# Output rows of a fused attention and ternary feed-forward kernel: the layer norm's gain applied with the deviation, its spread moved into the quantisation scalars, one step less between stages

## The reference

```python
z = out @ Wout
xh = (z - mean(z)) * rsqrt(var(z) + 1e-5) * g_out
act_scale = 127.0 / max(max(abs(xh)), 1e-5)
x_dq = clip(round(xh * act_scale), -128, 127) / act_scale
x = x + x_dq @ w.T + bias
```

## Time and profile before

| | |
|---|---|
| time, median of 3 runs | 1786.67 us (1785.74 to 1787.05) |
| the profiled execution's own time | 1786.81 us |
| its span, first to last instruction | 1784.5 us |
| TensorE busy | 1604.5 us, 90% |
| GpSimd busy | 1421.9 us, 80% |
| VectorE busy | 1407.2 us, 79% |
| ScalarE busy | 1141.8 us, 64% |

### The profile page before, as it was taken

How to read it: one execution, slowest core, us unless ns; L and a number is a source line. 1 busy time by engine, 2 the same in 40 slices (tenths; PEclk the granted TensorE clock), 3 DMA queues, 4 the chain that set the end, 5 groups by cost and what they waited for, 6 DMA issues and landing times.

```text
span 1784.5 us, 46777 instructions
## 1 busy us (share of the span) xinstructions
PE 1604.5 (90%) x15122; PEld 1079.6 (60%) x15122; DVE 1407.2 (79%) x2569; ACT 1141.8 (64%) x2195; POOL 1421.9 (80%) x934
## 2 busy tenths in 40 slices
PE   3786897899999999998995898799999999998997
PEld 1443554577777777776552455477777777776553
DVE  4885898788888888884765798688888888887576
ACT  1342555587787788777441555477887887787441
POOL 3564666799999999997673566799999999999574
PEclk9998999899999999998997999899999999999998
DMA  6000012011112111100023002021111111110023
GB/s 186 1 0 21 25 29 59 13 37 35 28 37 49 25 37 37 29 21 14 30 71 102 25 29 65 1 47 26 38 37 25 37 37 41 26 32 13 7 71 100
DMA packets 41302, 68.84 MB, mean 39 GB/s; under 512 B 8880, under 2 KB 9392, under 8 KB 41136
## 3 DMA queue, kind: packets, MB, share of 16 engines
q1 hardware_dynamic: 36512, 58.12, 13.3%
q10 hardware_dynamic: 4640, 8.54, 1.4%
HBM read 58.11 MB, written 8.54 MB: 37 GB/s over the span
## 4 chain that ended last, share of the span: by engine, by line
PE 44%; issue 26%; POOL 17%; DVE 9%; ACT 1%; DVEq 1%; POOLq 1%; DMA 1%; SPq 0%; ACTq 0%
PE ps L1162 21%; PE ps L1135 10%; PE ps L1138 10%; DVE work L930 5%; POOL rinv L491 4%; POOL work L496 4%; POOL work L523 3%; POOL qo L454 2%; POOL work L541 2%; PE ps L1204 1%; DVE work L958 1%; POOL rstd L486 1%; DVE denom L955 1%; POOL work L498 1%; POOL work L462 1%
## 5 line engine op out<-in xcount | busy, mean ns | idle before, releaser
L511 POOL TENSOR_TENSOR work<-work 128x1024 f16<-128x1024 f32 (+2 forms) x576 | 978.2, 1733 | 44.2 <-ACT work L644 41.6
L930 DVE SCALAR_TENSOR_TENSOR work<-ps,tab 128x1024 f32<-128x1024 f32 (+3 forms) x640 | 668.7, 1059 | 141.3 <-PE ps L1138 139.4
L644 ACT ACTIVATE work<-work 128x1024 f32<-128x1024 f32 (+3 forms) x640 | 578.2, 924 | 207.3 <-DVE work L930 203.4
L1162 PEld LDWEIGHTS ps<-vals,work 128*128 128x128 bf16 (+1 forms) x8704 | 545.3, 98 | 115.8 <-POOL work L511 2.2
L1162 PE MATMUL ps<-vals,work 128*128 128x129 f16 x8704 | 600.5, 221 | 1.9 <-POOL work L511 1.8
L1135 PE MATMUL ps<-qo,kT 128*128 128x512 f16 (+3 forms) x1280 | 344.2, 351 | 20.8 <-DVE work L930 15.0
L1138 PE MATMUL ps<-qo,kT 128*128 128x512 f16 (+3 forms) x1280 | 342.1, 349 | 0.0
L1106 PE MATMUL ps<-wq,work 128*128 128x512 f16 x768 | 178.0, 390 | 20.4 <-DVE work L863 20.4
L1138 PEld LDWEIGHTS ps<-qo,kT 128*128 128x128 f16 x1280 | 123.2, 98 | 117.5 <-issue 3.3
L1204 PE MATMUL ps<-wout,work 128*128 128x512 f16 x768 | 175.0, 385 | 0.0
L1106 PEld LDWEIGHTS ps<-wq,work 128*128 128x128 f16 x768 | 74.6, 100 | 113.5 <-issue 34.2
(11 more groups left out here) (131 smaller groups left out, 1727.0 us busy)
## 6 DMA issues: line engine op xcount, KB each, us to landing
tab<-bias_table SPq DMA_DIRECT2D x64, 512.0 KB, 4.7
work<-in_x SPq DMA_DIRECT2D x32, 256.0 KB, 2.6
tab<-in_x SPq DMA_DIRECT2D x32, 256.0 KB, 2.7
out_x<-work ACTq DMA_DIRECT2D x32, 256.0 KB, 2.2
work<-in_L_cond_Wq SPq DMA_DIRECT2D x1, 2048.0 KB, 12.8
work<-in_L_cond_Wout SPq DMA_DIRECT2D x2, 1024.0 KB, 10.3
qo<-in_L_cond_w SPq DMA_DIRECT2D x1, 1024.0 KB, 9.5
qo<-in_L_cond_b SPq DMA_DIRECT2D x2, 256.0 KB, 4.2
```

Of the source, the lines that this page charges most:

```text
L511: pool.tensor_tensor(low[:, k % LRING, :, c0:512], probs[:, r, :, c0:512], high[:, r, :, c0:512], ALU.subtract).then_inc(low_pool, 1)
L644: act.activation(probs[:, k % RING, :, c0:512], probs[:, k % RING, :, c0:512], ACT.Exp).then_inc(expd, 1)
L930: dve.scalar_tensor_tensor(out=probs[:, k % RING, :, c0:512], in0=ps[:, 2 * (k % 2):2 * (k % 2) + 2, c0:512], scalar=SCORE, in1=tab[:, :, ...
L1162: last = pe.matmul(ps[:, sum_bank(i, q), (t % SUMS) * VS:(t % SUMS + 1) * VS], parts[:, rings[part], e, s * P:(s + 1) * P], vals[:, j, :], ...
```

## The change

`c_norm` becomes one instruction that subtracts the mean from the PSUM bank and multiplies by g_out, and writes y directly. GpSimd's `c_gain` and the buffer zn go. y is now larger than before by the factor sqrt(var + eps), and so is its largest magnitude. Two one-number operations take rstd in: `amx` is max(amax * rstd, 1e-5), the same number as before, and `ascale` is 127 / amx * rstd. `c_power` also waits until the scale of the tile two before has been made, since that now reads the rstd buffer.

On VectorE `c_norm` is put right behind `c_stat`, and `c_quant` of the same tile goes at the end of the same step. The lags from `c_quant` on fall by one: quantisation 4 to 3, `c_turn_y` 5 to 4, `c_ternary` 6 to 5, `c_final` 7 to 6, `c_resid` 6 to 5, the store 8 to 7.

```diff
--- before.py
+++ after.py
...
-        zn = carve(work, D)
         y = carve(work, 2, D)
...
@@ -527,19 +526,15 @@
 
                 def c_power(t, u):
                     pool.wait_ge(c_ve, NT * b + t + 1)
+                    pool.wait_ge(c_as, NT * b + t + 1)
                     pool.tensor_tensor(rstd[:, u, :], ve[:, u, :], minus_half[:, 0:1],
                                        ALU.pow).then_inc(c_rstd, 1)
-
-                def c_gain(t, u):
-                    pool.wait_ge(c_zn, NT * b + t + 1 + 2)
-                    pool.wait_ge(c_y1, NT * b + t + 1)
-                    pool.tensor_tensor(y[:, u, :], zn, gout_b[:, :], ALU.mult).then_inc(c_y, 1)
 
                 def c_resid(t, u):
                     pool.wait_ge(c_xr[u], 8 * (NT * b + t - u) + 16)
                     pool.wait_ge(c_fin, NT * b + t + 1)
                     pool.tensor_tensor(xb[:, u, :], x_re[:, u, :], fbias_b[:, :], ALU.add).then_inc(c_xb, 1)
-                skewed(pool, NT, [(c_power, 3), (o_lows, 0), (c_gain, 3), (c_resid, 6)])
+                skewed(pool, NT, [(c_power, 3), (o_lows, 0), (c_resid, 5)])
 
 
         @block.scalar
@@ -706,7 +701,7 @@
                 def store(t, u):
                     act.wait_ge(c_fin, NT * b + t + 1 + 2)
                     act.dma_start(out[b, bass.ds((NT - 1 - t) * P, P), :], o_fin[:, u, :]).then_inc(c_out[u], 16)
-                skewed(act, NT, [(o_highs, 0), (c_turn, 1), (c_yturn, 5), (store, 8)], after_first=store_last)
+                skewed(act, NT, [(o_highs, 0), (c_turn, 1), (c_yturn, 4), (store, 7)], after_first=store_last)
             for u in range(2):
                 act.wait_ge(c_out[u], 16 * (B * NT // 2) + 16)
 
@@ -716,7 +711,7 @@
 
             for s, n in ((M[0]["n"], 2), (M[1]["n"], 2), (b_xn, 2), (b_v, 2), (b_qn, 2), (b_ss, 1),
                          (b_cd, 1), (b_xTl, 1), (b_snd, 1), (biased, CB), (o_added, 6), (c_y1, 2), (c_fin, 2),
-                         (c_zn, 2), (c_yq, 1), (M[1]["h"], 2), (bias_row, 2), (b_snp, 2), (wn_sum, 2)):
+                         (c_zn, 2), (c_as, 2), (c_yq, 1), (M[1]["h"], 2), (bias_row, 2), (b_snp, 2), (wn_sum, 2)):
                 dve.sem_inc(s, n)
 
             dve.wait_ge(ld_tern, 16)
@@ -998,25 +993,27 @@
 
                 def c_norm(t, u):
                     g = NT * b + t
-                    dve.wait_ge(c_rstd, g + 1)
-                    dve.wait_ge(c_y, g + 1)
-                    dve.tensor_scalar(zn, ps[:, 2 + u, :], mv[:, u, 0:1], rstd[:, u, :],
-                                      ALU.subtract, ALU.mult).then_inc(c_zn, 1)
+                    dve.wait_ge(c_mv, g + 1)
+                    dve.wait_ge(c_y1, g + 1)
+
+                    dve.scalar_tensor_tensor(out=y[:, u, :], in0=ps[:, 2 + u, :], scalar=mv[:, u, 0:1], in1=gout_b[:, :],
+                                             op0=ALU.subtract, op1=ALU.mult).then_inc(c_zn, 1)
 
                 def c_quant(t, u):
                     g = NT * b + t
-                    dve.wait_ge(c_y, g + 1 + 1)
+                    dve.wait_ge(c_zn, g + 1 + 2)
                     dve.tensor_reduce(amax[:, :], y[:, u, :], AX.X, ALU.max, apply_absolute_value=True
                                       ).then_inc(c_am, 1)
                     dve.wait_ge(c_am, g + 1)
-                    dve.tensor_scalar(amx[:, u, :], amax[:, :], 1e-5, None, ALU.max).then_inc(c_amx, 1)
+                    dve.wait_ge(c_rstd, g + 1)
+                    dve.tensor_scalar(amx[:, u, :], amax[:, :], rstd[:, u, :], 1e-5, ALU.mult, ALU.max).then_inc(c_amx, 1)
                     dve.wait_ge(c_amx, g + 1)
                     dve.reciprocal(arec[:, :], amx[:, u, :]).then_inc(c_rec, 1)
                     dve.tensor_scalar(rowscale[:, bass.ds(t, 1)], amx[:, u, :], dequant[:, 0:1], None, ALU.mult
                                       ).then_inc(c_rs, 1)
                     dve.wait_ge(c_rec, g + 1)
-                    dve.tensor_scalar(ascale[:, :], arec[:, :], 127.0, None, ALU.mult).then_inc(c_as, 1)
-                    dve.wait_ge(c_as, g + 1)
+                    dve.tensor_scalar(ascale[:, :], arec[:, :], 127.0, rstd[:, u, :], ALU.mult, ALU.mult).then_inc(c_as, 1)
+                    dve.wait_ge(c_as, g + 1 + 2)
                     dve.tensor_scalar(y1, y[:, u, :], ascale[:, 0:1], 127.0, ALU.mult, ALU.min
                                       ).then_inc(c_y1, 1)
                     dve.wait_ge(c_y1, g + 1 + 2)
@@ -1034,7 +1031,7 @@
                     dve.scalar_tensor_tensor(out=o_fin[:, u, :], in0=ps[:, 5 + u, :],
                                              scalar=rowscale[:, bass.ds(t, 1)], in1=xb[:, u, :],
                                              op0=ALU.mult, op1=ALU.add).then_inc(c_fin, 1)
-                skewed(dve, NT, [(c_stat, 3), (c_final, 7), (c_quant, 4), (c_norm, 3)])
+                skewed(dve, NT, [(c_stat, 3), (c_norm, 3), (c_final, 6), (c_quant, 3)])
 
 
         @block.tensor
@@ -1222,7 +1219,7 @@
                         last = pe.matmul(ps[:, 5 + u, :], yT[:, u, c, :], ternT[:, c, :], start=c == 0,
                                          stop=c == KC - 1)
                     last.then_inc(c_f, 1)
-                skewed(pe, NT, [(c_turn, 1), (c_turn_y, 5), (c_ternary, 6), (c_project, 2)])
+                skewed(pe, NT, [(c_turn, 1), (c_turn_y, 4), (c_ternary, 5), (c_project, 2)])
 
 
 _INS = ["x", "cond_64", "mask_BxS_bf1", "L0_cond_g_norm", "L0_cond_Wq", "L0_cond_Wkv", "L0_cond_q_scale",
```

More of the change, by code:

```diff
@@ L332, in build @@
         low_dve, low_pool, b_vh, b_snp = (sem(n) for n in ("low_dve", "low_pool", "b_vh", "b_snp"))
-        c_high, c_low, c_T, c_Tc, c_z, c_st, c_mv, c_ve, c_rstd, c_zn, c_y, c_am, c_amx, c_rec, c_as, c_rs = (
+        c_high, c_low, c_T, c_Tc, c_z, c_st, c_mv, c_ve, c_rstd, c_zn, c_am, c_amx, c_rec, c_as, c_rs = (
             sem(n) for n in ("c_high", "c_low", "c_T", "c_Tc", "c_z", "c_st", "c_mv", "c_ve", "c_rstd", "c_zn",
-                             "c_y", "c_am", "c_amx", "c_rec", "c_as", "c_rs"))
+                             "c_am", "c_amx", "c_rec", "c_as", "c_rs"))
         c_y1, c_y2, c_yq, c_yT, c_yTc, c_f, c_xb, c_fin = (sem(n) for n in (
@@ L414, in _ @@
         def _(pool):
-            for s, n in ((M[0]["g"], 1), (M[1]["g"], 1), (b_lo, 4), (c_y, 1), (c_xb, 2)):
+            for s, n in ((M[0]["g"], 1), (M[1]["g"], 1), (b_lo, 4), (c_xb, 2)):
                 pool.sem_inc(s, n)
```

## The result

The changed kernel takes 1774.28 us (median of 6 runs, 1773.26 to 1774.94), the kernel before on the same chip 1785.83 us (1784.12 to 1787.05). The ratio is 0.9938, 95% interval 0.9928 to 0.9948: 11.5 us less where 11.1 were forecast, inside the range, and no run of the one kernel reaches a run of the other. The profiled execution took 1774.26 us, its span is 1772.5 us.

What follows compares the result with a forecast made beforehand. TensorE was taken to bound the middle, so only the two drains pay: 5.4 + 5.4 + 0.3 = 11.1 us off 1786.81 gives 1775.7, median 1775.6 us. Own range 1772.5 to 1779; with rivals 1 and 2, 1772 to 1781.5.

Steps and rivals of the forecast that it cites:

- The middle is covered: Third stage's middle steps: TensorE stays without gaps at 7.16 us a step, so VectorE and GpSimd changes cost 0.
- The norm: VectorE's subtract and multiply out of PSUM in each step: 0.75 us instead of 0.81, bounds 0.6 and 1.0.
- The second scalars: VectorE's two one-number operations each take a second scalar: together 0.05 us, bounds 0 and 0.2.
- The port: In each drain the first pass over y waits for GpSimd's residual 14: 0.26 us, bounds 0 and 1.3.
- T to Y: Each drain, from start of the last tile's statistics (T) to start of its transposes (Y): 12.11 us falls to 5.63.
- 1.09 us ahead of T: One group of transposes and ternary matmuls moves ahead of the last projection, delaying T by 1.09 us per drain.
- The clock: Second pass's drain: one idle time instead of two may leave the first matmuls after it at 2.4 GHz, saving 0.3 us.
- The first drain: Stores and loads still collide behind Y, final operation 6 us after Y; the whole 5.4 us carries into the next pass.
- Rival 2: First drain pays more: reloads and stores spread wider, final operation 2.85 us behind Y, not 6.05; 1772.4 us, chance 0.12.
- GpSimd's busy time: Removing the gains cuts GpSimd's busy time by 32 x 1.27 = 41 us, with no time for it.
- Rivals 1 and 4: Rival 1: only one drain pays, 1781.0 us, chance 0.13. Rival 4: Y comes no earlier, 1786.7 us, chance 0.05.
- Rival 3: Middle no longer covered: VectorE's step passes 7.16 us through waits for GpSimd; 1790 or 1804 us, chance 0.08.

Runs made afterwards that it cites:

- e5: The changed kernel with two more reductions of the projection's PSUM bank in each VectorE step, ahead of the norm, results unread; 1776.11 us.
- e6: The changed kernel with four more reductions of the projection's PSUM bank in each VectorE step, ahead of the norm, results unread; 1808.69 us.
- e2: The kernel before with the changed order and lags but the old arithmetic, the gain on GpSimd put ahead of the low parts; 1807.06 us.
- e3: The changed kernel with all stages behind the quantisation kept at the lags of the kernel before; 1773.06 us.
- e11: The changed kernel with residual and store first, final operation last, old lags for TensorE and y copy, plus ten unread matmuls a pass; 1768.87 us.
- e12: As e11, but with the store back at the end of ScalarE's step; 1768.63 us.
- e7: The changed kernel with GpSimd's residual listed ahead of its power and low parts; 1773.16 us.
- e8: The changed kernel with the store at the head of ScalarE's step, not behind the copy of y; 1772.30 us.
- e9: The changed kernel again, unedited, on another chip at a later time; 1773.23 us.
- e1: The changed kernel's arithmetic with the order and lags of the kernel before; 1779.81 us.

## Why the prediction was right

- *The middle is covered.* Right: 20.00 of 20.00 us busy, 7.16 us a step. The worst case of GpSimd beside the passes over y was nearly what happens in each step: the first pass is 1.55 us. e5 and e6 set the edge where the prediction had it, and e2 shows what lies beyond.
- *The norm* at 0.75 us: 0.75. *The second scalars* at 0.05 us, bounds 0 and 0.2: from the reduction to the first pass 1763.32 - 1761.91 = 1.41 against 1.29, so 0.12. The norm begins 1.16 us behind T and not 1.25, which gives it back. *The port* at 0.26: the pass took 0.70 and not 0.49, 0.21. *T to Y* at 5.63: 5.57.
- *1.09 us ahead of T.* Right: from the first tile's statistics to T 1.09 and 1.08 us more, and e3 has the 1.09 us back in both passes.
- *The clock* at 0.3 us: wrong, 0. The granted clock stayed at 1.00 until about 1764 and fell in the idle time, ahead of Y:

```profile
1760.50:1763.00 2.50, 0.00 (x0) 0.00 (x0) 2.42 (x7) 0.00 (x0) 2.26 (x3) 1.00 0.28 105
1763.00:1765.00 2.00, 0.00 (x0) 0.00 (x0) 1.90 (x7) 0.00 (x0) 0.74 (x1) 0.78 0.38 130
1765.00:1767.00 2.00, 2.00 (x8) 1.00 (x9) 0.61 (x1) 0.59 (x1) 1.25 (x1) 0.50 0.19 71
```

  The step that failed is that one idle time in place of two leaves the first matmuls behind it at 2.4 GHz. In e11, where TensorE had work until 1758.2, the clock was 1.00 up to Y, and in e12 throughout, so the term exists. In the last drain of e7 TensorE idled 4.30 us and not 4.52, and the eight matmuls took 3.13 us and not 3.62, but the clock had fallen ahead of Y there as well:

```profile
1763.30:1765.30 2.00, 1.93 (x8) 1.01 (x9) 0.67 (x2) 0.58 (x1) 1.18 (x1) 0.50 0.15 55
```

  It rose again during them (0.68 in 1765.0 to 1767.0). The first drain of e7 has the same 4.30 us of idle time and took 3.62 us, and e2, with 6.34 us idle, took 3.22. So e7's shorter time comes from the clock's rise behind Y and not from a later fall, and the length of the idle time does not order these cases. What decides when it rises is open.
- *The first drain.* The collision of stores and loads stayed, as said, but it held less: the forecast sign, 6 us from Y to the final operation, did not come. Tile 14's came 3.98 us behind Y and tile 15's 6.33, where before the two came back to back from 6.05 us on. Y to the next pass became 0.55 us shorter where it was taken as unchanged. Rival 2's mechanism is real and was not in the change: in e8 and e12 Y to the next pass is 7.58 and 6.67 us, against 9.39.
- *GpSimd's busy time* fell by 39.9 us (1421.9 to 1382.0) and was worth nothing as such, as said (41).
- *The sum* was 11.1 us against the profiled execution of before, and the two executions differ by 12.55. The 1.45 more are 0.1 from T to Y, 0.55 behind Y in the first drain, 0.55 outside the span, 0.56 by which the time ahead of the first statistics was shorter, less the 0.3 of the clock. Of these only the first is of the change for certain: behind Y in the first drain two profiles of the changed kernel differ by 0.25 us themselves (9.39, and 9.14 in e9). The medians differ by 11.5. T to Y and the 1.09 us give 2 x (12.11 - 5.57 - 1.09) = 10.9 of them. That the forecast is within half a us owes something to luck: the 0.3 us of the clock did not come, and the 0.55 behind Y, which were not forecast, stand in their place.
- *The range.* The execution's own range went down to 1772.5, but the terms named for its lower end, 0.3 us more in each of two drains, give 1775.0. The lower end rests on rival 2 alone.
- Rivals 1 and 4 fell with the move of the next pass (971.29 to 965.35). Rival 3 is what e2 and e6 do.

The 11.5 us are thus two drains. Of them 5.1 are the arithmetic's alone (e1); the other 6.4 come from the order within VectorE's step, since e3, with that order and the old lags, has them too. The one form of the order tried with the old arithmetic loses 22 us (e2).

## What to carry to other kernels

Where one engine fills the middle of a pipelined stage, look at the drain: count from the last tile's first dependent operation to the last tile's final one, and see what of other tiles stands in between on each queue. Work hidden in the middle can be worth its full time there; here the order within a step counted and the lag did not. Before moving work to a covered engine, find the edge of the cover, in which waits for another engine may be swallowed by real work, as in e5. Order changes that each help can meet in one in-order queue: read the timeline of the combination.

## What the runs showed of the hardware that was not expected

VectorE's scaling pass over y (SBUF to SBUF), where it starts in the same moment as a GpSimd instruction, ends behind all of it: 1.55 us and not 0.49. The norm, out of PSUM, took 0.75 us in all 32 tiles, with GpSimd's power beginning beside it (at 1704.35 in the step above), and the reduction of y, beside the low parts, 0.67 to 0.69. In e2 a waiting pass was served between two GpSimd instructions (it ended 0.28 us behind the low parts) and the residual of GpSimd, begun meanwhile, took 1.45 us and not 1.27. Ten matmuls a pass whose results nothing reads made the kernel faster by 2.6 us. And one store of 256 KB took 4.0 us to land (e7), where the median is 2.0, with no load beside it, only the store ahead of it and then a few small packets.
